# Third layer of a four-layer recurrent network: four PSUM banks for the attention scores, three for the ring

## The chip, the cores and the metric

The kernel runs on one core of a Trainium2 chip. The metric is the device time of one execution in microseconds (us). It stands for a whole network: four layers, each with an attention part and a feed-forward part, computed for four sequences ("rows") of 1024 tokens with 128 channels each.

PSUM, the memory that TensorE (PE) writes its products to, has eight banks per partition. One bank holds 128 x 512 float32 values, which is one product as this kernel makes them. ScalarE (ACT) and VectorE (DVE) read the banks. GpSimd (POOL) prepares masks and copies in SBUF.

## The reference, cut to what matters

The change touches the third layer. What it computes for each row `x` of 1024 tokens:

```python
xn = _layernorm(x, axis=-1)
s = _L2_attn_ref(xn, Wq, bq, Wk, bk, Wv, bv, Wo, bo, W1, b1, W2, b2, g1, beta1, g2, beta2)
g = _silu(_L2_ffn_ref(xn, gate_w, gate_b, w1, b1, w2, b2))
x = x + s * g

# the attention of _L2_attn_ref: 16 heads of 8 channels, full (no mask), rotary positions
q, k = apply_rope(heads(h @ Wq + bq)), apply_rope(heads(h @ Wk + bk))   # h: x normalised again
scores = q @ k.T / sqrt(8)
attn = softmax(scores) @ v

# _L2_ffn_ref: a switch layer, 8 experts with 80 places each
expert = argmax(softmax(tokens @ gate_w + gate_b))      # one expert for a token
dispatch = einsum('nec,nd->ecd', places, tokens)        # tokens into the experts' places
h = gelu(einsum('ecd,edf->ecf', dispatch, w1) + b1)
out = einsum('nec,ecd->nd', places * prob, einsum('ecf,efd->ecd', h, w2) + b2)
```

## The kernel before, in words

The first three layers each run `attention_layer`, which computes all four rows of a layer in one program for all engines. Nothing of its order is decided at run time. Each engine has several streams of work (generators); every item has a planned time, and `weave` puts the items of all streams of an engine into one sequence by these times. On the chip each engine then executes its sequence in order and waits on semaphores.

**Batches and blocks.** The heads of a row are taken in groups of four, and the queries in halves of 512, which makes 8 batches a row and 32 in the layer. A batch in the third layer has 8 blocks; a block is 128 keys against 512 queries, for four heads. For each head of a block PE makes a 128 x 512 product of scores in a bank of `ps_st`, ACT takes its exponential into `prob` (L1356), and PE multiplies `prob` with the values into the bank `ps_o` (L1254, eight matmuls for a block, "the values' product").

**Pairs.** The third layer uses a form of the operands in which two heads lie in different halves of PE's rows (`form.groups == 2`, in the code `paired`). PE works on two heads at a time where both are free to start. A pair of scores is four matmuls: two of L1267 (`score`) and two of L1274 (`score_apart`), which add the remaining terms. A block has two pairs; below they are called A (heads n = 0, 1) and B (n = 2, 3). The values' product of block b - 1 is planned between pair A and pair B of block b.

**Maxima.** The exponentials need the maximum of each query's scores, one batch ahead. PE computes the scores of the next batch once more the other way round (L1327, 128 queries x 512 keys, 32 of them for a batch, "fills", also in pairs), and DVE takes the maximum of each over its row (L1389, `TENSOR_REDUCE mhalf<-mx`). About four fills go with a block. After the last fill of a batch comes the turn of the maxima (L1339, kind "max"), and DVE makes three bf16 parts of it, which a DMA puts beside the queries (`qs<-neg`).

**The ring.** Fills share their banks, the tile `mx`, with everything else that PE makes for DVE or ACT in the meantime: the turned output of a batch (L1343, kind "out"), the arrival of the next row (L859, L685, L681), and the products of the switch layer (L1788 logits, L2460 counts, L2467 dispatch, L2474, L2486 hidden, L2495 second product, L2505 combination). All these products, in the order of their planned times, are the list `ring`; item i uses bank `i % RING`, and before it PE waits until item `i - RING` has been read (`open_bank`). The function `by` moves the reading of a switch product on DVE and ACT ahead of the planned time of item `slot + RING`, so that no engine waits for something behind itself.

**Scores' banks.** Score u (four for a block, counted through the layer) uses bank `u % 3` of `ps_st` and waits for the exponential of score u - 3 (`score_bank`). Both scores of a pair must be free before the two can run side by side.

Banks in the layer before: three for the scores, one for `ps_o`, four for the ring.

Of the kernel before, what the change touches and what calls it, by code (L numbers as in the profile page):

```python
# [20 lines left out]
ACT = mybir.ActivationFunctionType  # L21
# [3 lines left out]
P = 128  # L25
NT = T // P
HALF = 512
NH, DH = 16, 8
GH = 4
# [161 lines left out]
class Net:  # L191
# [32 lines left out]
    n = 0  # L224
# [160 lines left out]
PROBS = 3  # L385
# [612 lines left out]


NEG, NEG_NARROW = 5.0, 7.0  # L1000
RING = 4


def attention_layer(net, mode, scale, proj, ffns, arrivals=(), departures=()):
# [7 lines left out]
    nc = net.nc  # L1012
    rows = len(ffns)
    form = net.form
    R = form.rows
    paired = form.groups == 2
    heads_in_turn = (0, 2, 1, 3) if paired else (0, 1, 2, 3)
    batches = [(g, hf) for g in range(NG * rows) for hf in range(2)]
    NB = len(batches)
# [8 lines left out]
    for e, (g, hf) in enumerate(batches):  # L1028
        opens.append(len(blocks))
        for kt in range(NT):  # L1030
            lo, hi = queries_of(kt)
            q0, q1 = max(lo, hf * HALF), min(hi, (hf + 1) * HALF)
# [144 lines left out]
    with net.phase("att", names + proj.names + several) as (S, blk):  # L1177
        net.stale_next = net.stale_next + ffns[-1].used_up
        qs, ks, prob, vst, mhalf, mrow, neg, nrest, osb, rec = (net.qs, net.ks, net.prob, net.vst, net.mhalf, net.mrow, net.neg,
                                                                net.nrest, net.osb, net.rec)  # L1180
        ps_st = net.psum("ps_st", [P, 3, HALF])
        ps_o = net.psum("ps_o", [P, HALF])
        mx = net.psum("mx", [P, RING, HALF])
        proj.start(S, [ps_st[:, 0, :], ps_st[:, 1, :]], [mx[:, 2, :], mx[:, 3, :]], [ps_st[:, 2, :], ps_o[:, :]])
        proj.after = turn_max_at(0) + 1.1
        for r in range(rows):
            ffns[r].calm = [clock.at(y) + 0.8 for y in of_row[r][:-1]]
# [15 lines left out]
        def open_bank(pe, *item):  # L1203


            i = slot[item]
            if i >= RING:
                _, kind, e, n = ring[i - RING]
                if kind in FED:
                    sem, value = ffns[e].read(kind, n)  # L1210
                    pe.wait_ge(sem, value)
                else:
                    pe.wait_ge(S["mx_used"], place[kind, e, n])
            elif proj.rope and i >= 2:
                pe.wait_ge(S["s"], 1 + i)
            return mx[:, i % RING, :]

        for f in ffns:
# [24 lines left out]
        def scores(pe):  # L1243
# [12 lines left out]
                last.then_inc(S["summed"], 1)  # L1256

            def score_bank(u):
                if u >= 3:
                    pe.wait_ge(S["exped"], u - 2)  # L1260
                return ps_st[:, u % 3, :]

            def score(b, n, stop):
                e, kt, q0, q1 = blocks[b]
# [5 lines left out]
            def score_apart(b, n):  # L1270
                e, kt, q0, q1 = blocks[b]
                g = batches[e][0]
                row, lane = form.lane(heads_in_turn[n])
                return nc.tensor.matmul(ps_st[:, (GH * b + n) % 3, 0:q1 - q0], net.kx[row:row + 64, g % 2, lane, kt * P:(kt + 1) * P],  # L1274
                                        net.qx[row:row + 64, g % 2, q0:q1], start=False, stop=True)

            for b, (e, kt, q0, q1) in enumerate(blocks):
                for n in range(GH):
                    yield score_at(b, n)
                    if b == opens[e] and n == 0:  # L1280
                        pe.wait_ge(S["neg_landed"], negs * (e + 1))
                    if b == 0 and n == 0:
                        pe.wait_ge(S["value"], 4)
                        pe.wait_ge(S["vout"], 2)
                        if paired:
                            pe.wait_ge(S["apart"], 16 * 3 * GH)
                    if paired and n % 2 == 0:
                        score(b, n, False)
                        score(b, n + 1, False)
                        score_apart(b, n).then_inc(S["scores"], 1)  # L1290
                        score_apart(b, n + 1).then_inc(S["scores"], 1)
                    if not paired:
                        masks = score_masks(kt, q0, q1)
                        last = score(b, n, not masks)
                        for j, (m, a, z, c0, c1) in enumerate(masks):
                            last = nc.tensor.matmul(ps_st[:, (GH * b + n) % 3, c0:c1], net.ident_bf, m[:, a:z], start=False,  # L1296
                                                    stop=(j == len(masks) - 1))
                        last.then_inc(S["scores"], 1)
                    if n == (1 if paired else 3) and b >= 1:
                        yield values_at(b - 1)  # L1300
                        values(b - 1)
# [44 lines left out]
        def exponentials(act):  # L1346
            for b, (e, kt, q0, q1) in enumerate(blocks):
                for n, h in enumerate(heads_in_turn):
                    u = GH * b + n
                    yield score_at(b, n)  # L1350
                    act.wait_ge(S["scores"], u + 1)
                    if u == 0:
                        act.wait_ge(S["p3"], 4)
                    if n == 0 and b >= PROBS:
                        act.wait_ge(S["summed"], b - PROBS + 1)
                    nc.scalar.activation(prob[:, b % PROBS, h, 0:q1 - q0], ps_st[:, u % 3, 0:q1 - q0], ACT.Exp,  # L1356
                                         scale=scale).then_inc(S["exped"], 1)
                if b >= 1 and b - 1 == closes[blocks[b - 1][0]]:
                    yield from take_output(act, blocks[b - 1][0])
            yield from take_output(act, NB - 1)  # L1360
# [2424 lines left out]
```

## Time and profile before

| | us |
|---|---|
| median of 3 runs (lowest, highest) | 4225.28 (4214.74, 4245.58) |
| the profiled execution | 4225.9 |
| its span | 4223.9 |
| PE, DVE, ACT, POOL busy in the span | 3664.7, 2647.4, 2149.2, 864.8 |

The page of the profile gives the busy time of each engine in the span. Of the lines named above, it lists L1356 (ACT), L1389 (DVE), L1327, L1267 and L1254 (PE) as the five costliest groups of the program; the first two layers use them too. In the third layer the scores run from 1720.7 to 2800.2 us. The rows further down are all from there. In a row of the timeline the first number is the start, the second the length of a merged run of like instructions, `x2` their count, and the bracket at the end says how long the engine sat idle before them and which instruction ended that.

### The profile page before, as it was taken

Reading aid. Unit: us, or ns where it says so; the run is one execution under the profiler, and the core shown is the slowest. Engines: PE = TensorE matmul, PEld = TensorE weight load, DVE = VectorE, ACT = ScalarE, POOL = GpSimd, SP = SyncE. Lnnn points to the kernel's source line nnn. Section 1 sums busy time; section 2 is a strip of 40 time slices with the busy share of each in tenths; the row PEclk is TensorE's granted clock in tenths of the full one; section 3 lists DMA queues with packets and bytes.
Section 4 is the critical chain, followed back from the end, with each engine's and each line's share of the span. In section 5 each row is a group of like instructions: output and inputs, shape, how many; then the busy total and the mean of one; then the engine's idle time right before and its main releaser. Section 6 shows DMA issues by size and latency. Waiting matters only on the chain. (4 is left out here: it accounts for less than half of the span.)

```text
span 4223.9 us, 77424 instructions
## 1 busy us (share of the span) xinstructions
PE 3664.7 (87%) x28760; PEld 2040.5 (48%) x28760; DVE 2647.4 (63%) x5977; ACT 2149.2 (51%) x4957; POOL 864.8 (20%) x1071
## 2 busy tenths in 40 slices
PE   5988978888989995899898898989888898888987
PEld 3655654444545543333333333345555665555565
DVE  5667646565555654777677777737555665665765
ACT  3555554554555453465565655653554554444454
POOL 1111000000010002122233132124212331431421
PEclk8999988988999898899999999999999999999999
DMA  3212311101101102111011011002120230321212
GB/s 111 61 46 43 75 27 46 40 22 44 24 18 44 29 13 85 35 32 39 18 44 32 24 39 32 23 31 63 36 72 23 61 81 8 80 60 29 56 41 54
DMA packets 149533, 183.37 MB, mean 43 GB/s; under 512 B 34568, under 2 KB 102216, under 8 KB 145832
## 3 DMA queue, kind: packets, MB, share of 16 engines
q1 hardware_dynamic: 143268, 171.01, 15.5%
q10 hardware_dynamic: 5892, 7.41, 0.7%
q8 instruction: 230, 3.77, 0.4%
q14 instruction: 143, 1.17, 0.1%
HBM read 91.69 MB, written 34.08 MB: 30 GB/s over the span
## 5 line engine op out<-in xcount | busy, mean ns | idle before, releaser
L1356 ACT ACTIVATE prob<-ps_st 128x512 f32<-128x512 f32 (+3 forms) x2432 | 1123.5, 510 | 1146.6 <-PE ps_st L1296 577.9
L1389 DVE TENSOR_REDUCE mhalf<-mx 128x1 f32<-128x512 f32 (+3 forms) x2064 | 1256.7, 653 | 589.1 <-PE mx L1330 316.5
L1327 PE MATMUL mx<-ks,qs 56*128 56x512 bf16 (+4 forms) x2304 | 648.7, 365 | 125.9 <-DVE g_tok L1964 52.6
L1267 PE MATMUL ps_st<-qs,ks 59*128 59x512 bf16 (+4 forms) x2432 | 678.1, 350 | 82.5 <-ACT prob L1356 69.9
L1254 PE MATMUL ps_o<-prob,vst 128*32 128x512 f32 (+3 forms) x5376 | 566.7, 504 | 2.7 <-ACT osb L1367 1.5
L1267 PEld LDWEIGHTS ps_st<-qs,ks 75*128 75x128 bf16 (+1 forms) x2432 | 206.3, 98 | 504.9 <-ACT prob L1356 356.0
L1327 PEld LDWEIGHTS mx<-ks,qs 72*128 72x128 bf16 (+1 forms) x2304 | 199.9, 100 | 390.5 <-DVE mhalf L1389 86.4
L1439 POOL COPY vst<-v_tok 128x256 f32<-128x256 f32 x48 | 19.8, 416 | 1137.9 <-PE ps_o L1254 1137.4
L3312 ACT ACTIVATE o<-ps,nm,lrq 128x128 f32<-128x128 f32 x512 | 227.1, 459 | 35.3 <-DVE nm L3427 24.0
L1274 PE MATMUL ps_st<-qx,kx 64*128 64x512 bf16 x1024 | 241.7, 386 | 0.0
L1254 PEld LDWEIGHTS ps_o<-prob,vst 128*32 128x32 f32 x5376 | 113.8, 110 | 165.7 <-issue 65.9
L2377 POOL TENSOR_SCALAR ffn_small<-bcs,table 80x128 f32<-80x128 f32 x256 | 148.6, 598 | 124.4 <-PE mx L2505 113.5
L2022 PE MATMUL mx<-stream 128*128 128x128 f32 x1024 | 155.1, 294 | 0.4 <-DVE mhalf L1389 0.2
L2022 PEld LDWEIGHTS mx<-stream 128*128 128x128 f32 x1024 | 138.3, 203 | 31.0 <-issue 21.7
L1296 PE MATMUL ps_st<-band_kq_bf,ident_bf 128*128 128x128 bf16 (+2 forms) x1024 | 149.7, 218 | 0.0
L3380 DVE SCALAR_TENSOR_TENSOR o<-ps,stream,tabs 128x512 f32<-128x512 f32 x128 | 94.6, 744 | 67.3 <-ACT ctx_tok L3282 27.1
L1330 PE MATMUL mx<-band_qk_bf,ident_bf 128*128 128x134 bf16 (+2 forms) x960 | 134.7, 222 | 0.0
L1995 PE MATMUL mx<-xn_ch,stream 128*128 128x512 f32 x256 | 120.7, 619 | 4.3 <-ACT stream L1981 4.3
L3093 PE MATMUL ps<-xn_ch,stream 128*128 128x512 f32 x256 | 120.9, 594 | 3.5 <-DVE xn_ch L3368 3.5
L253 PE MATMUL pt<-ident_bf 128*128 128x512 bf16 x336 | 95.7, 423 | 28.7 <-ACT o L3312 28.7
L1296 PEld LDWEIGHTS ps_st<-band_kq_bf,ident_bf 128*128 128x128 bf16 x1024 | 102.3, 100 | 26.2 <-issue 7.6
L1296 PE MATMUL ps_st<-later_kq_bf,ident_bf 128*128 128x128 bf16 x512 | 112.2, 233 | 0.0
(488 smaller groups left out, 6563.1 us busy)
## 6 DMA issues: line engine op xcount, KB each, us to landing
qs<-q_scr SPq DMA_DIRECT2D x186, 96.0 KB
ks<-k_scr SPq DMA_DIRECT2D x90, 192.0 KB
lkt<-o SPq DMA_DIRECT2D x256, 64.0 KB, 2.0
lve<-lv SPq DMA_DIRECT2D x24, 512.0 KB, 4.6
lqt<-o SPq DMA_DIRECT2D x160, 64.0 KB, 2.0
tabs<-local_tables SPq DMA_DIRECT2D x4, 2048.0 KB, 8.6
k_scr<-part SPq DMA_DIRECT2D x30, 256.0 KB, 3.2
lqt<-o ACTq DMA_DIRECT2D x96, 64.0 KB, 2.1
```

The source lines that it names most:

```text
L1254: last = nc.tensor.matmul(ps_o[32 * h:32 * h + 32, a - hf * HALF:z - hf * HALF], vst[:, g % 2, kt, h, :], prob[:, b % PROBS, h, a - q0:z - ...
L1267: return nc.tensor.matmul(score_bank(GH * b + n)[:, 0:q1 - q0], ks[g % 2][row:row + R + 3, lane, kt * P:(kt + 1) * P], qs[g % 2][row:row + ...
L1274: return nc.tensor.matmul(ps_st[:, (GH * b + n) % 3, 0:q1 - q0], net.kx[row:row + 64, g % 2, lane, kt * P:(kt + 1) * P], net.qx[row:row + ...
L1296: last = nc.tensor.matmul(ps_st[:, (GH * b + n) % 3, c0:c1], net.ident_bf, m[:, a:z], start=False, stop=(j == len(masks) - 1))
L1327: last = nc.tensor.matmul(bank[:, j * w:(j + 1) * w], qs[g % 2][row:row + R, hf, lane, (t - 4 * hf) * P:(t - 4 * hf + 1) * P], ks[g % 2][r ...
L1330: last = nc.tensor.matmul(bank[:, j * w + c0:j * w + c1], net.ident_bf, m[:, a:z], start=False, stop=(k == len(masks) - 1))
L1356: nc.scalar.activation(prob[:, b % PROBS, h, 0:q1 - q0], ps_st[:, u % 3, 0:q1 - q0], ACT.Exp, scale=scale).then_inc(S["exped"], 1)
L1389: nc.vector.tensor_reduce(mhalf[:, hf, h0:h0 + heads, t - 4 * hf, part], bank[:, 0:heads * (k1 - k0)].rearrange("p (n w) -> p n w", n=head ...
L2022: last = nc.tensor.matmul(bank[:, t * C:(t + 1) * C], self.h[:, i, j, t * P:(t + 1) * P], W(f"l1_w2_{e}", self.HB, j), start=(j == 0), sto ...
L2377: last = nc.gpsimd.tensor_scalar(self.sec_t[:, t % 2, e, :], self.bcs[:, t * P:(t + 1) * P], net.K("slot_id")[0:CAP, e:e + 1], None, ALU.i ...
L3093: last = nc.tensor.matmul(pab[:, n % 2, s, :], W(f"l3_wqkv{d}")[:, c0:c0 + P], ch[:, i * HALF:(i + 1) * HALF], start=True, stop=True)
L3312: nc.scalar.activation(pr[:, g, i, :], ps[:, t % 2, g, i, :], ACT.Exp, bias=nm[:, g, i:i + 1], scale=norm[t][:, i // 2, g, i % 2:i % 2 + 1 ...
```

## The change

In the third layer, and only there (`paired`), the scores get four banks and the ring three; the first two layers keep three and four. Of the projection's second products, one moves from `mx` into the fourth bank of `ps_st`. The first use of the third bank of `mx` and the first score wait until all four of these products have been read (`S["s"]`, 4).

```diff
-RING = 4
+BANKS = 7
...
+    SB = 4 if paired else 3
+    RING = BANKS - SB
...
-        ps_st = net.psum("ps_st", [P, 3, HALF])
+        ps_st = net.psum("ps_st", [P, SB, HALF])
         ps_o = net.psum("ps_o", [P, HALF])
         mx = net.psum("mx", [P, RING, HALF])
-        proj.start(S, [ps_st[:, 0, :], ps_st[:, 1, :]], [mx[:, 2, :], mx[:, 3, :]], [ps_st[:, 2, :], ps_o[:, :]])
+        proj.start(S, [ps_st[:, 0, :], ps_st[:, 1, :]], [ps_st[:, 3, :], mx[:, 2, :]] if paired else [mx[:, 2, :], mx[:, 3, :]], [ps_st[:, 2, :], ps_o[:, :]])
...
             elif proj.rope and i >= 2:
-                pe.wait_ge(S["s"], 1 + i)
+                pe.wait_ge(S["s"], 4 if paired else 1 + i)
             return mx[:, i % RING, :]
...
             def score_bank(u):
-                if u >= 3:
-                    pe.wait_ge(S["exped"], u - 2)
-                return ps_st[:, u % 3, :]
+                if u >= SB:
+                    pe.wait_ge(S["exped"], u - SB + 1)
+                return ps_st[:, u % SB, :]
...
                         if paired:
                             pe.wait_ge(S["apart"], 16 * 3 * GH)
+                            pe.wait_ge(S["s"], 4)
...
-                    nc.scalar.activation(prob[:, b % PROBS, h, 0:q1 - q0], ps_st[:, u % 3, 0:q1 - q0], ACT.Exp,
+                    nc.scalar.activation(prob[:, b % PROBS, h, 0:q1 - q0], ps_st[:, u % SB, 0:q1 - q0], ACT.Exp,
                                          scale=scale).then_inc(S["exped"], 1)
```

PE, ACT, POOL and SP keep the order of their instructions. On DVE `by` now looks three items ahead, so that some readings of switch products move forward past one or two reductions, or past the reading of an "out". DVE's order in the second row, around the first dispatch copy (L2417; in the changed kernel the same instruction is L2420, L1389 is L1392, L1415 and L1421 are L1418 and L1424). Before:

```order
L1389 TENSOR_REDUCE mhalf<-mx 128x1 x12
L1415 RECIPROCAL rec<-mx 128x16
L1421 TENSOR_TENSOR tabs<-mx,rec 128x4x32
L2417 COPY ffn_small<-mx 128x160
L1389 TENSOR_REDUCE mhalf<-mx 128x1 x8
```

With the change:

```order
L1392 TENSOR_REDUCE mhalf<-mx 128x1 x12
L2420 COPY ffn_small<-mx 128x160
L1418 RECIPROCAL rec<-mx 128x16
L1424 TENSOR_TENSOR tabs<-mx,rec 128x4x32
L1392 TENSOR_REDUCE mhalf<-mx 128x1 x8
```

The copy moved ahead of the two readings of the turned output, because the "out" is now the item that needs the copy's bank.

PE's order at the start of the layer, where the projection's second products (L444) are made. Before:

```order
L442 MATMUL ps_st<-in_ch,w 128x512
L444 MATMUL mx<-in_ch,w 128x512
L442 MATMUL ps_st<-in_ch,w 128x512
L444 MATMUL mx<-in_ch,w 128x512
L442 MATMUL ps_st<-in_ch,w 128x512
```

With the change:

```order
L442 MATMUL ps_st<-in_ch,w 128x512
L444 MATMUL ps_st<-in_ch,w 128x512
L442 MATMUL ps_st<-in_ch,w 128x512
L444 MATMUL mx<-in_ch,w 128x512
L442 MATMUL ps_st<-in_ch,w 128x512
```

Every other second product goes to the new bank of `ps_st`; nothing changed its place.

## Rows read from the trace of the kernel before

**Rows 1.** Busy time by engine, 1720 to 2815 us; granted clock, DMA share, GB/s last.

```profile
1720.00:2815.00 1095.00, 988.59 (x6760) 372.29 (x6761) 763.51 (x1591) 642.35 (x1244) 278.29 (x428) 0.98 0.11 33
```

**Rows 2.** Waits, same stretch: who waited for whom, total us, times, longest.

```profile
PE ps_st L1267 <- ACT prob L1356: 49.1, 139, 3.1
...
ACT prob L1356 <- PE ps_st L1274: 490.0, 322, 53.0
```

**Rows 3.** Timeline, one block with four fills and nothing else.

```profile
2126.10 0.39 PE L1267 MATMUL ps_st<-qs,ks 59*128 59x512 bf16 x2
...
2126.54 0.38 PE L1327 MATMUL mx<-ks,qs 56*128 56x512 bf16 x2
2126.74 1.09 ACT L1356 ACTIVATE prob<-ps_st 128x512 f32<-128x512 f32 x2 [0.46 <-PE ps_st L1274]
2126.76 0.38 PE L1267 MATMUL ps_st<-qs,ks 59*128 59x512 bf16 x1
2126.96 2.58 DVE L1389 TENSOR_REDUCE mhalf<-mx 128x1 f32<-128x512 f32 x4 [0.46 <-PE mx L1327]
2127.39 0.39 PE L1267 MATMUL ps_st<-qs,ks 59*128 59x512 bf16 x1 [0.25 <-ACT prob L1356]
...
2127.62 0.59 PE L1327 MATMUL mx<-ks,qs 56*128 56x512 bf16 x2
...
2128.14 1.07 PE L1254 MATMUL ps_o<-prob,vst 128*32 128x512 f32 x8
...
2129.14 0.39 PE L1267 MATMUL ps_st<-qs,ks 59*128 59x512 bf16 x2
```

**Rows 4.** Timeline, one block of the last batch, which has no fills.

```profile
2791.75 0.39 PE L1267 MATMUL ps_st<-qs,ks 59*128 59x512 bf16 x2
...
2793.04 0.39 PE L1267 MATMUL ps_st<-qs,ks 59*128 59x512 bf16 x1 [0.47 <-ACT prob L1356]
...
2793.58 1.07 PE L1254 MATMUL ps_o<-prob,vst 128*32 128x512 f32 x8
2794.57 0.39 PE L1267 MATMUL ps_st<-qs,ks 59*128 59x512 bf16 x2
```

**Rows 5.** Timeline, one block with six fills, four of them together.

```profile
1762.87 0.39 PE L1267 MATMUL ps_st<-qs,ks 59*128 59x512 bf16 x2
...
1763.73 3.18 DVE L1389 TENSOR_REDUCE mhalf<-mx 128x1 f32<-128x512 f32 x5 [0.47 <-PE mx L1327]
...
1764.39 1.07 PE L1327 MATMUL mx<-ks,qs 56*128 56x512 bf16 x4
1765.40 1.07 PE L1254 MATMUL ps_o<-prob,vst 128*32 128x512 f32 x8
1766.40 0.39 PE L1267 MATMUL ps_st<-qs,ks 59*128 59x512 bf16 x2
```

**Rows 6.** Timeline, a dispatch product's copy behind an "out" (second row).

```profile
2021.03 1.29 DVE L1389 TENSOR_REDUCE mhalf<-mx 128x1 f32<-128x512 f32 x2 [2.47 <-PE mx L1327]
2021.93 0.66 PE L1343 MATMUL mx<-table,osb 128*128 128x128 f32 x4
...
2023.12 0.31 DVE L2417 COPY ffn_small<-mx 128x160 f32<-128x160 f32 x1
...
2023.49 0.39 PE L1327 MATMUL mx<-ks,qs 56*128 56x512 bf16 x2 [0.37 <-DVE ffn_small L2417]
```

**Rows 7.** Line L1327, same stretch as Rows 1: what ended PE's idle time before.

```profile
  DVE mhalf L1389: 30.3, 79
  DVE tabs L2433: 29.5, 36
  DVE xn_ch L2426: 15.9, 29
```

**Rows 8.** Timeline, a row's arrival (square root on ACT), and after a hidden window.

```profile
2056.42 0.60 PE L1267 MATMUL ps_st<-qs,ks 59*128 59x512 bf16 x1 [3.12 <-ACT prob L1356]
...
2148.67 0.39 PE L1267 MATMUL ps_st<-qs,ks 59*128 59x512 bf16 x1 [1.30 <-ACT prob L1356]
```

More of the change, by code:

```diff
@@ L1273, in score_apart @@
                 row, lane = form.lane(heads_in_turn[n])
-                return nc.tensor.matmul(ps_st[:, (GH * b + n) % 3, 0:q1 - q0], net.kx[row:row + 64, g % 2, lane, kt * P:(kt + 1) * P],
+                return nc.tensor.matmul(ps_st[:, (GH * b + n) % SB, 0:q1 - q0], net.kx[row:row + 64, g % 2, lane, kt * P:(kt + 1) * P],
                                         net.qx[row:row + 64, g % 2, q0:q1], start=False, stop=True)
@@ L1295, in scores @@
                         for j, (m, a, z, c0, c1) in enumerate(masks):
-                            last = nc.tensor.matmul(ps_st[:, (GH * b + n) % 3, c0:c1], net.ident_bf, m[:, a:z], start=False,
+                            last = nc.tensor.matmul(ps_st[:, (GH * b + n) % SB, c0:c1], net.ident_bf, m[:, a:z], start=False,
                                                     stop=(j == len(masks) - 1))
```

## The prediction

> **What bounds the kernel now.** I read the busy time by engine over the third layer first, then the waits of PE and ACT there, then the timeline of single blocks, and last what ends PE's idle time before the fills. Only the third layer changes. In its 1095 us PE is busy for 989, DVE for 764 and ACT for 642 [rows 1]. PE is the engine nearest to its limit, but its busy time does not show how many matmuls ran side by side. The waits show where banks are short: a score waited for an exponential 139 times, 49.1 us in all, and ACT in turn waited 490.0 us for scores [rows 2]. The two wait for each other in a loop.
>
> The loop is read in a block that has only its four fills [rows 3]. I count from the start of pair B, 2126.10. B's fills start at 0.44. ACT starts B's two exponentials at 0.64 and is through at 1.73. The first score of pair A starts at 0.66, the second only at 1.29, when the first exponential has ended (1.19) and 0.10 has passed. A's fills follow at 1.52, the second of them 0.21 later (0.59 for two of 0.38), the values' product at 2.04, the next pair B at 3.04. The 0.63 between the two scores of A is what the missing bank costs: A0 runs alone for 0.38, then PE idles for 0.25. The values' product takes 1.00 and starts 0.31 after the last fill.
>
> **The fourth bank.** With it the second score of A needs an exponential that is long past, so A runs as a pair at 0.66 and its fills could start at 1.10. But the values' product needs B's exponentials, ready at 1.73 + 0.10 = 1.83. The last batch shows that loop without any fills: there the second score of A waits as well, and the values' product starts at 2793.58 - 2791.75 = 1.83 and the next block at 2.82 [rows 4]. So a block can't go below 2.83, and of the 0.63 given back at A only 0.21 is left where the block is plain. In blocks where a product of the switch layer or of the arrival stands between A and the values' product, exponentials are done in time and the whole 0.63 is returned.
>
> **The third ring bank.** A pair of fills (i, i + 1) needed the reads of i - 4 and i - 3, both of the pair before last. Now its second fill needs the read of i - 2, the first fill of the pair just before. In the plain block DVE starts the first read at 0.86 and needs 2.58 / 4 = 0.645 for each [rows 3]; PE goes on 0.06 after a read (2023.12 + 0.31 to 2023.49, [rows 6]). The second of A's fills can thus start at 0.86 + 0.645 + 0.06 = 1.57, the values' product at 1.88, the next block at 2.88 in place of 3.04. DVE needs 2.58 of these, so it keeps up. **Gain 0.16 a block; by my count over the layer's timeline 58 blocks are of this kind: 9.3 us.**
>
> **Blocks with other work behind A.** I count 35 in which A split by 0.63 and neither the exponentials nor the ring hold the values' product afterwards: 35 x 0.63 = 22 us. In 21 more a part comes back, about 0.35 each: 7.4 us. Together with the plain ones these are 114 blocks, against 139 waits [rows 2].
>
> **Blocks with four fills in a row.** I count 46, about half behind pair A and half behind pair B. In the one shown, A's fills start at 1.52, all four run through, and the values' product starts at 2.53, the next block at 3.53 [rows 5]. With three banks the four fills follow the reads one by one. DVE reads B's fills from 0.86 to 2.15 and A's first to 2.80; A's second fill starts at 1.57, the third at 2.15 + 0.06 = 2.21, the fourth at 2.80 + 0.06 = 2.86, the values' product at 3.17. That is 0.64 later than before, in a block that before also had its 0.63 split: all of that is already set off. Worked out for four fills behind B I get the same, one read more. It isn't made up later, since the following block without fills was held by the exponentials anyway. **Loss 46 x 0.64 = 29 us.**
>
> **Switch and arrival products.** Behind a long product, the first fill of a pair now waits for its read instead of the second; they then start together, which costs nothing. It costs where a single item follows. The "out" of 2021.93 used a free bank; now it must wait for the copy, which DVE takes up behind two reductions: 2021.03 + 1.29 + 0.31 + 0.06 = 2022.69, 0.76 later [rows 6]. The bound from below is nothing (the earlier start of PE covers it), from above one read and a copy, 0.96. I take 0.65 and 20 such places: **13 us**. The eight windows of hidden products lose a bank as well, and a fill behind them waits for one more GELU, but ACT must first load the table for the exponentials, which held the second score of A for 1.30 [rows 8]: nothing. If that cover were gone, 0.9 each, 7 us.
>
> **Arrivals.** While ACT works on the square root of an arriving row, PE stands for 3.12 us [rows 8]. With four banks pair B and its fills pass before PE stops, some 0.65 to 1.3 us earlier in the end; three arrivals, 3 us.
>
> **The start of the layer.** The third fill bank and the first score wait for the last sine product's read; the keys' transfers that the fills need come later. Nothing.
>
> Sum: -9.3 - 22 - 7.4 - 3 + 29 + 13 = +0.3. In one stretch of five blocks that I worked through in turn the result was 0.1 us slower, where the terms above give about zero, because a PE that is earlier meets the same DVE; I add 2 us. Against the profiled execution of 4225.9, which lies 0.6 above the median of the runs, this gives **4228 us, no change.**
>
> **Rivals.**
>
> *Faster, the fourth bank pays and the ring has slack* (0.15). DVE is idle for 30% of the layer [rows 1], and its lag behind PE may be taken up by an earlier start of the fills. Then the 29 and 13 us shrink to a few, and what is left is 42 plus the 0.05 a plain block in which the ring and not the exponentials decides (3): 4225.9 - 45 = 4181. Against it: at 79 fills PE already stood until DVE's reduction with four banks [rows 7]. It holds if fewer than about 15 of the 46 blocks lose a read.
>
> *All of the split comes back* (0.03). Every one of the 139 waits returns its idle time and the 0.38 in which one score ran alone: 49.1 + 139 x 0.38 = 102, 4124 us. Against it speak the blocks of the last batch [rows 4], whose period the bank doesn't set. The Trainium skill has this as its rule: "Perfetto Trace Analysis", Optimization Strategy, takes the same gap repeating on the engine that should be saturated as a sign that SBUF or PSUM is too small for the next tile. By it the sum would be the 102 us; the trace agrees with it on where the gap is and, in the last batch, not on its worth.
>
> *Slower, the ring becomes the bound* (0.20). PE's idle time before a fill was ended 79 times by a reduction, 36 times by the reading of a combination product and 29 times by that of a second product [rows 7]. If every one of these 144 places waits for one more read, each before a values' product, the loss is 144 x 0.645 = 93 us in place of 42, less the 42 gained: 4225.9 + 51 = 4277. It decides where DVE is behind by a read or more when a pair of fills comes. It speaks for this rival that a stall splits the pair of fills, so that they run one after the other; against it, that such a pair was mostly split before, and then nothing is added.
>
> *Neither bank matters* (0.05): the exponentials' loop holds everywhere and DVE's lag is absorbed: 4226.
>
> **Chances.** The forecast itself has 0.57. A change within 1%, 42 us, is what I call no change, about what a measurement of this kernel can tell. Faster by over 1%: 0.15, most of the two faster cases. Slower by over 1%: 0.20. Within: 0.65. The range goes from the first faster case to the slower one, 4180 to 4275.
>
> **What the profile after would show.** Waits of scores for exponentials nearly gone, pairs A at 0.66 behind B; plain blocks at 2.88; four fills in a row spread over some 1.3 us more, with waits for DVE's reductions before L1327 up several times; the blocks of the last batch still at 2.82. I am wrong if plain blocks stay at 3.04 or go to 2.83 with four fills unspread, or if the waits before fills exceed what the scores gave back by more than 40 us.

## The result, and the profile after

The changed kernel takes 4264.27 us (median of 9 runs, 4255.67 to 4278.19), the kernel before 4229.10 beside it (9 runs, 4212.58 to 4245.58). The ratio is 1.0088, 95% interval 1.0066 to 1.011: slower by 0.9%, 35 us. The forecast was 4228, no change. By the prediction's bound of 1% it is no change, but the interval shows a loss, and the time lies nearer to the slower rival (4277) than to the forecast. One execution of all those below, of the first kernel with short reads, took 10497 us at a mean granted clock of 0.388 and is left out of every time.

The profiled execution after has a span of 4257.0, against 4223.9. I cut the third layer of both traces into its 255 blocks, from one pair A to the next. Their sum is 30.7 us longer (1077.2 before), and the layer's start lies 2.3 later, so the two differ where the change was made. Busy time by engine as in [rows 1], over the layer's blocks from its first pair A:

```profile
1723.02:2830.92 1107.90, 972.95 (x6696) 374.52 (x6698) 757.59 (x1565) 620.99 (x1229) 274.74 (x426) 0.97 0.11 33
```

PE is idle for 1107.90 - 972.95 = 135 us of the layer. The same view of the kernel before, from its first pair A:

```profile
1720.68:2797.85 1077.17, 977.08 (x6696) 366.51 (x6696) 758.05 (x1566) 633.40 (x1229) 275.80 (x426) 0.98 0.12 33
```

There it was idle for 100. So 35 us of idle time were added and 4 of busy time went. Who waited for whom after, as [rows 2] (L1267 has become L1269, L1274 L1276, L1254 L1256, L1327 L1330, L1356 L1359, L1389 L1392; PEld is PE's weight load):

```profile
PEld mx L1330 <- DVE mhalf L1392: 136.4, 230, 1.8
...
PE mx L1330 <- DVE mhalf L1392: 35.2, 96, 1.3
```

Before, the scores' wait for exponentials stood there with 139 times and 49.1 us. Now it is the fills that wait, 96 times for 35.2 us. A matmul of a fill had waited for a reduction only this often:

```profile
PE mx L1327 <- DVE mhalf L1389: 2.3, 11, 0.2
```

The exchange is plainest in the idle time before each matmul line (busy and mean | idle before, and what ended it). Before, from 1720 to 2815:

```profile
L1254 PE MATMUL ps_o<-prob,vst 128*32 128x512 f32 x2048 | 281.4, 622 | 2.7 <-ACT osb L1367 1.5 <-ACT prob L1356 1.2
L1267 PE MATMUL ps_st<-qs,ks 59*128 59x512 bf16 x1024 | 271.6, 391 | 53.7 <-ACT prob L1356 49.1 <-DMA qs<-neg 3.2 <-DVE mhalf L1389 1.1
L1327 PE MATMUL mx<-ks,qs 56*128 56x512 bf16 x984 | 241.3, 387 | 32.7 <-DVE tabs L2433 9.5 <-DVE bcs L2422 6.3 <-DVE ffn_small L2417 4.3
```

and after, from 1720 to 2831, since the layer now ends later:

```profile
L1256 PE MATMUL ps_o<-prob,vst 128*32 128x512 f32 x2032 | 281.6, 627 | 16.7 <-ACT prob L1359 13.2 <-ACT osb L1370 3.5
L1330 PE MATMUL mx<-ks,qs 56*128 56x512 bf16 x988 | 266.8, 392 | 90.8 <-DVE mhalf L1392 35.2 <-DVE tabs L2436 13.9 <-DVE xn_ch L2429 9.3
L1269 PE MATMUL ps_st<-qs,ks 59*128 59x512 bf16 x1022 | 209.6, 393 | 5.4 <-DMA qs<-neg 3.2 <-ACT prob L1359 1.9
```

The scores gave back 53.7 - 5.4 = 48.3. The fills took 90.8 - 32.7 = 58.1, and the values' products 16.7 - 2.7 = 14.0. The same view gives 6.1 before the hidden products (L2489) and 4.2 before the "out" (L1346), where it gave 0.2 and 0.8 before. Together that is 33 of the 35 us. Line L1330, what ended the idle time before its matmuls and weight loads, where [rows 7] had 79, 36 and 29 times:

```profile
  DVE mhalf L1392: 171.6, 326
  DVE tabs L2436: 40.5, 36
  DVE xn_ch L2429: 27.7, 26
```

**The plain block** [rows 3], rows of PE and of its weight load:

```profile
2135.54 0.39 PE L1269 MATMUL ps_st<-qs,ks 59*128 59x512 bf16 x2
...
2136.21 0.38 PE L1269 MATMUL ps_st<-qs,ks 59*128 59x512 bf16 x2
...
2136.65 0.89 PE L1330 MATMUL mx<-ks,qs 56*128 56x512 bf16 x2
2137.15 0.09 PEld L1330 LDWEIGHTS mx<-ks,qs 56*128 56x128 bf16 x1 [0.62 <-DVE mhalf L1392]
...
2137.47 1.06 PE L1256 MATMUL ps_o<-prob,vst 128*32 128x512 f32 x8
...
2138.47 0.39 PE L1269 MATMUL ps_st<-qs,ks 59*128 59x512 bf16 x2
```

Pair A runs undivided at 0.67 behind B. A's first fill starts at 1.11, the second waits for a read, the values' product starts at 1.93 and the next pair B at 2.93. It was 3.04.

**Four fills in a row** [rows 5]. This pair B began at 1735.97:

```profile
1737.08 0.89 PE L1330 MATMUL mx<-ks,qs 56*128 56x512 bf16 x2
1737.58 0.09 PEld L1330 LDWEIGHTS mx<-ks,qs 56*128 56x128 bf16 x1 [0.62 <-DVE mhalf L1392]
1738.18 0.09 PEld L1330 LDWEIGHTS mx<-ks,qs 56*128 56x128 bf16 x1 [0.51 <-DVE mhalf L1392]
...
1738.77 0.09 PEld L1330 LDWEIGHTS mx<-ks,qs 56*128 56x128 bf16 x1 [0.50 <-DVE mhalf L1392]
...
1739.10 1.06 PE L1256 MATMUL ps_o<-prob,vst 128*32 128x512 f32 x8
1740.09 0.39 PE L1269 MATMUL ps_st<-qs,ks 59*128 59x512 bf16 x2
```

One fill now follows each read, 0.6 apart. The values' product stands at 3.13 where it stood at 2.53, the next pair B at 4.12 (3.53). Over the layer, the 46 blocks with four fills in a row hold 59 of the waits of a fill for a reduction, with 22.9 of the 35.2 us; before they held one, of 0.2.

**The last batch** [rows 4], without fills:

```profile
2827.69 0.39 PE L1269 MATMUL ps_st<-qs,ks 59*128 59x512 bf16 x2
...
2829.47 1.06 PE L1256 MATMUL ps_o<-prob,vst 128*32 128x512 f32 x8 [0.73 <-ACT prob L1359]
2830.47 0.39 PE L1269 MATMUL ps_st<-qs,ks 59*128 59x512 bf16 x2
```

2.78 from B to B, where it was 2.82: the exponentials hold it, and the wait only moved from the score to the values' product.

**An "out"** [rows 6] now waits for the copy ahead of it (first row below). **An arrival** [rows 8], where the longest wait had been 3.12, now has two waits of 1.34 and 0.51:

```profile
2033.13 0.66 PE L1346 MATMUL mx<-table,osb 128*128 128x128 f32 x4 [0.61 <-DVE ffn_small L2420]
...
2067.39 0.39 PE L1330 MATMUL mx<-ks,qs 56*128 56x512 bf16 x1 [1.34 <-DVE mhalf L1392]
...
2068.28 0.88 PE L1269 MATMUL ps_st<-qs,ks 59*128 59x512 bf16 x2 [0.51 <-ACT prob L1359]
```

**A hidden window.** PE now stands inside it:

```profile
2154.13 1.28 ACT L2451 ACT_TABLE_LOAD   x1
...
2156.46 1.88 PE L2489 MATMUL mx<-ffn_small,stream 128*128 128x80 f32 x8 [1.47 <-ACT ffn_small L2451]
...
2159.26 1.93 PE L1256 MATMUL ps_o<-prob,vst 128*32 128x512 f32 x8
```

There are four hidden products in a window, and a GELU for each. With three banks the fourth uses the bank of the first, so it waits for the first GELU, and that comes behind a table load. Afterwards the values' product takes 1.93 and not 1.06. The granted clock (third number from the end) in and behind this window shows why it is longer:

```profile
2152.00:2157.00 5.00, 3.53 (x29) 3.30 (x28) 1.04 (x2) 4.97 (x12) 1.16 (x1) 0.96 0.05 12
2157.00:2159.00 2.00, 2.00 (x9) 1.33 (x8) 0.08 (x1) 2.00 (x11) 1.15 (x1) 0.50 0.00 0
2159.00:2161.00 2.00, 2.00 (x9) 0.20 (x8) 1.20 (x2) 1.82 (x4) 0.00 (x0) 0.50 0.00 0
2161.00:2163.00 2.00, 2.00 (x14) 0.74 (x11) 0.38 (x1) 0.81 (x2) 0.00 (x0) 0.50 0.00 0
```

Of PE's two levels, 2.4 and 1.2 GHz, it had the lower for some 6 us from the end of the stall on. The block took 10.81 us; in the kernel before the same block took 8.28, at a clock of 1.00 throughout.

By kind of block, before to after, in us:

| kind (its make-up before) | blocks | difference (each rounded) |
|---|---|---|
| four fills in a row | 46 | +26.4 |
| four fills in two pairs, nothing else | 93 | +6.1 |
| one with only the turn of the maxima | 10 | -0.9 |
| with hidden products | 8 | +8.7 |
| all others (other products, "out", last batch) | 98 | -9.5 |
| sum | 255 | +30.7 |

Two of the three blocks in which an arriving row's square root stops PE have the make-up of plain ones and stand among the 93, the third stands among the 46.

### The profile page after: what moved, and what is told of

It reads as the page before. It is cut to its first block and busy times, and to the rows that moved or that the text cites. A ratio compares the mean times of both kernels' runs of the same rounds, so it can differ in the third digit from the quotient of the medians.

```text
span 4257.0 us, 77424 instructions
## 1 busy us (share of the span) xinstructions
PE 3661.3 (86%) x28760; PEld 2049.0 (48%) x28760; DVE 2646.9 (62%) x5977; ACT 2135.6 (50%) x4957; POOL 863.6 (20%) x1071
## 5 line engine op out<-in xcount | busy, mean ns | idle before, releaser
L1359 ACT ACTIVATE prob<-ps_st 128x512 f32<-128x512 f32 (+3 forms) x2432 | 1110.0, 512 | 1187.7 <-PE ps_st L1299 573.3
L1392 DVE TENSOR_REDUCE mhalf<-mx 128x1 f32<-128x512 f32 (+3 forms) x2064 | 1251.3, 651 | 618.5 <-PE mx L1333 317.8
L1330 PE MATMUL mx<-ks,qs 56*128 56x512 bf16 (+4 forms) x2304 | 673.1, 367 | 183.9 <-DVE g_tok L1967 52.0
L1269 PE MATMUL ps_st<-qs,ks 59*128 59x512 bf16 (+4 forms) x2432 | 616.3, 350 | 35.0 <-ACT prob L1359 22.7
L1256 PE MATMUL ps_o<-prob,vst 128*32 128x512 f32 (+3 forms) x5376 | 567.7, 505 | 18.6 <-ACT prob L1359 15.1
L1330 PEld LDWEIGHTS mx<-ks,qs 72*128 72x128 bf16 (+1 forms) x2304 | 199.8, 100 | 514.1 <-DVE mhalf L1392 199.5
L1269 PEld LDWEIGHTS ps_st<-qs,ks 75*128 75x128 bf16 (+1 forms) x2432 | 190.2, 98 | 377.1 <-ACT prob L1359 211.4
L1276 PE MATMUL ps_st<-qx,kx 64*128 64x512 bf16 x1024 | 207.0, 387 | 0.0
L1256 PEld LDWEIGHTS ps_o<-prob,vst 128*32 128x32 f32 x5376 | 113.9, 110 | 164.6 <-issue 67.8
L3383 DVE SCALAR_TENSOR_TENSOR o<-ps,stream,tabs 128x512 f32<-128x512 f32 x128 | 94.5, 743 | 67.2 <-ACT ctx_tok L3285 27.3
L253 PE MATMUL pt<-ident_bf 128*128 128x512 bf16 x336 | 95.2, 421 | 29.6 <-ACT o L3315 29.6
L1333 PEld LDWEIGHTS mx<-band_qk_bf,ident_bf 128*128 128x128 bf16 x960 | 96.5, 101 | 31.6 <-issue 5.7
```

What stands on the lines that cost most here:

```text
L1256: last = nc.tensor.matmul(ps_o[32 * h:32 * h + 32, a - hf * HALF:z - hf * HALF], vst[:, g % 2, kt, h, :], prob[:, b % PROBS, h, a - q0:z - ...
L1269: return nc.tensor.matmul(score_bank(GH * b + n)[:, 0:q1 - q0], ks[g % 2][row:row + R + 3, lane, kt * P:(kt + 1) * P], qs[g % 2][row:row + ...
L1276: return nc.tensor.matmul(ps_st[:, (GH * b + n) % SB, 0:q1 - q0], net.kx[row:row + 64, g % 2, lane, kt * P:(kt + 1) * P], net.qx[row:row + ...
L1330: last = nc.tensor.matmul(bank[:, j * w:(j + 1) * w], qs[g % 2][row:row + R, hf, lane, (t - 4 * hf) * P:(t - 4 * hf + 1) * P], ks[g % 2][r ...
L1333: last = nc.tensor.matmul(bank[:, j * w + c0:j * w + c1], net.ident_bf, m[:, a:z], start=False, stop=(k == len(masks) - 1))
L1392: nc.vector.tensor_reduce(mhalf[:, hf, h0:h0 + heads, t - 4 * hf, part], bank[:, 0:heads * (k1 - k0)].rearrange("p (n w) -> p n w", n=head ...
```

## The experiments

The kernel before ran beside each group of them (medians of 17 to 23 runs: 4227.28, 4227.56, 4226.31 us); ratios are to those runs. A single trace can differ from the median, since layers 1 and 2, which are the same code, end between 1705 and 1736 us in these traces. So times are compared by ratio, and the traces only by the blocks of layer 3.

### The change taken apart: the ring alone, the order alone

The ring of three alone. The eighth bank holds nothing but products of the projection at the start (against the changed kernel, cut to the sizes):

```diff
-    SB = 4 if paired else 3
-    RING = BANKS - SB
+    SB = 3
+    RING = 3 if paired else 4
```

> The third layer with three banks for the scores and three for the ring; the eighth bank holds nothing but two of the projection's sine products. The engines' orders are those of the changed kernel, so against the changed kernel this takes away the fourth score bank alone, and against the kernel before it shows the ring alone. Theory (the ring of three costs, the fourth score bank returns little, because the exponentials and the reads of the fills hold the values' product anyway): the split of pair A is back (about 139 waits), and the time is 15 to 35 us above the changed kernel, 1.2 to 1.7% above before. Rival (the two effects are separate and each large): the ring alone costs 33 + 68 = 100 us, 2.4% above before. Rival (the fourth bank returns nothing at all): the same time as the changed kernel within 5 us.

Measured: 4285.01 us, ratio 1.0131 (1.0114 to 1.0149). That is 21 us above the changed kernel, as the theory had it.

The order alone: four ring banks and three for scores, but DVE's readings placed as for a ring of three (against the kernel before; ACT's order stays as it was):

```diff
-        i = slot[item] + RING
+        i = slot[item] + (3 if paired else RING)
```

> The kernel before with its banks (three and four), but with the look-ahead of the order set to three in the third layer, so that DVE has the order of the changed kernel: some readings of switch products come one or two reductions earlier. Theory (the missing bank costs, not the order): within 3 us of before. Rival (DVE now waits for switch products with reductions behind it, and that is the loss): 15 to 33 us slower.

Measured: 4214.11 us, ratio 0.9971 (0.9956 to 0.9986). This is slightly faster than the kernel before, which I had not seen coming.

The three traces add up over the layer's blocks as follows:

| step | four fills | plain | max | hidden | other | sum | by medians |
|---|---|---|---|---|---|---|---|
| order for a ring of three | -3.3 | -3.9 | 0.0 | +1.4 | -1.4 | -7.2 | -13 |
| ring of three | +38.1 | +12.7 | -0.5 | +12.1 | +8.2 | +70.6 | +71 |
| fourth score bank | -8.5 | -2.7 | -0.4 | -4.8 | -16.3 | -32.7 | -21 |

So the ring bank is worth two to three and a half times the score bank, whose worth is known only beside a ring of three. The score bank gives half its gain in blocks with other work and next to nothing in plain ones. In the run with the ring alone (1718 to 2861 us) both waits stand side by side:

```profile
PE ps_st L1270 <- ACT prob L1360: 44.5, 140, 2.7
PE mx L1331 <- DVE mhalf L1393: 28.2, 81, 0.8
```

### Is it the length of DVE's reads?

Both kernels, with DVE reading 256 of the 512 columns, so that half of the keys are left out of the maxima:

```diff
-                                            bank[:, 0:heads * (k1 - k0)].rearrange("p (n w) -> p n w", n=heads),
+                                            bank[:, 0:256].rearrange("p (n w) -> p n w", n=1) if paired else
+                                            bank[:, 0:heads * (k1 - k0)].rearrange("p (n w) -> p n w", n=heads),
```

> The kernel before, but in the third layer each of DVE's reductions reads 256 of the 512 columns of its bank, so that half of the keys are left out of the maxima; a read takes about 0.38 us instead of 0.645. It is the base for the next kernel. Theory (DVE's reads set the pace at the places with four fills and behind the long products): 20 to 40 us faster than before. Rival (the loop of scores and exponentials alone sets the pace with four ring banks): within 10 us of before.

> The changed kernel with the same short reads (half of the keys left out of the maxima). Against the short-read version of before it shows the change where the ring has slack. Theory (the loss is DVE's reads against three banks): the loss turns into a gain, 15 to 45 us faster than the short-read version of before, with plain blocks at 2.83 us. Rival (the loss comes from something else that the change brings, the order or the clock): still 15 us or more slower than the short-read version of before.

Measured: 4174.83 us with the banks before (median of six; 0.9871, 0.9851 to 0.9891) and 4176.58 with the changed banks (0.988, 0.9866 to 0.9895). The first gained more than the 20 to 40 us expected. With short reads the change costs nothing, so its loss of 35 us hangs for the most part on the time of the reads. But it doesn't gain the 15 to 45 us of the theory either. To see why, one more execution of the first, for its trace:

> The run with short reads on the banks before, once more for its trace (it leaves half the keys out of the maxima). Its time was 4178 against 4177 on the changed banks. Theory 1 (with short reads the score bank's gain is there, and what eats it is waits for products' copies and GELUs, which are not shortened): plain blocks stay at 3.04 against 2.83 on the changed banks, and the changed banks lose as much in blocks with products and hidden windows, 8 us or more in the latter. Rival (with short reads the fills get through so early that the split of A no longer sets anything): plain blocks at 2.83 here as well.

Measured: 4167.17 us in one run. A read now took 418 ns instead of 684. Idle time before the lines, short reads, banks before, from 1711 us, where this layer starts:

```profile
L1389 DVE TENSOR_REDUCE mhalf<-mx 128x1 f32<-128x256 f32 x984 | 366.2, 418 | 349.6 <-PE mx L1327 346.5 <-DVE neg L1408 1.5
L1254 PE MATMUL ps_o<-prob,vst 128*32 128x512 f32 x2048 | 277.0, 613 | 3.1 <-ACT osb L1367 1.8 <-ACT prob L1356 1.2
L1267 PE MATMUL ps_st<-qs,ks 59*128 59x512 bf16 x1024 | 272.7, 388 | 56.3 <-ACT prob L1356 46.1 <-DMA qs<-neg 6.0 <-DVE mhalf L1389 3.8
...
L1327 PE MATMUL mx<-ks,qs 56*128 56x512 bf16 x984 | 223.9, 383 | 17.5 <-DVE tabs L2434 4.3 <-DVE bcs L2423 4.2 <-ACT ffn_small L2449 4.2
```

and short reads with the changed banks:

```profile
L1256 PE MATMUL ps_o<-prob,vst 128*32 128x512 f32 x2048 | 278.0, 615 | 25.7 <-ACT prob L1359 15.5 <-ACT osb L1370 7.1
L1330 PE MATMUL mx<-ks,qs 56*128 56x512 bf16 x992 | 245.2, 388 | 41.7 <-DVE tabs L2437 10.1 <-DVE mhalf L1392 9.0 <-DVE xn_ch L2430 6.5
L1269 PE MATMUL ps_st<-qs,ks 59*128 59x512 bf16 x1024 | 208.6, 390 | 8.2 <-DMA qs<-neg 6.3 <-ACT prob L1359 1.6
```

The scores give back 48.1. The fills lose 24.2, most of it no longer to reductions but to the copies and sums of products, which were not shortened, and the values' products lose 22.6, mostly to the exponentials. By kind, from the banks before to the changed ones: four fills +7.2, plain -4.1, hidden +8.1, other -19.3, max -0.3, sum -8.5. The typical plain block went from 3.04 to 2.78, the hidden windows still lost 8. The first theory stands in these two points, but not in the blocks with other products, which gained 19. The sum of -8.5 is one trace against one, while the medians differ by 2; in part it can be the clock, since the layer had the lower level for 25 us in the first trace and for 37 in the second.

### Four fills in a row, taken apart

Fills dealt out at three places of a block instead of two, on the changed banks, on those before, and on those before with the look-ahead of three, which gives the same order as the first:

```diff
-            return clock.at(starts[b] + (0.5 * int(2 * (at - starts[b]) / lasts[b]) + 0.22) * lasts[b])
+            return clock.at(starts[b] + (0.22, 0.45, 0.72)[int(3 * (at - starts[b]) / lasts[b])] * lasts[b])
```

> The banks of the changed kernel; fills are dealt out at three places of a block instead of two, so that four in a row no longer occur. Theory 1 (the loss of the ring of three lies in the 46 blocks with four fills in a row, 0.57 us each): 26 us come back, 4238 us, and PE's waits for DVE's reductions before the fills fall from 96 to under 40. Rival (each pair of fills anywhere pays one read, since DVE reads a fill in 0.645 and the ring holds no more than one and a half reads): the waits stay at 90 or more, and the time is within 8 us of the 4264 of the changed kernel.

> The same three places for the fills, with the banks of the kernel before. Theory 1 (with four banks a run of four fills costs nothing): within 8 us of the kernel before, 4220 to 4236. Rival (spreading by itself gives 10 us or more, as fills then stand between B's scores and A's): 4217 or less; what the thirds do on three banks would then have to be counted less this gain.

> The banks of the kernel before, fills at three places of a block, and the order made with a look-ahead of three: instruction for instruction the order of the run with thirds on the changed banks, so the two differ by their banks alone. The same pair without thirds lies 50 us apart (4214 and 4264). Theory 1 (some 26 us of that are the blocks with four fills in a row): the pair with thirds lies 15 to 30 us apart, this kernel at 4222 to 4236. Rival (the read of the newest pair is paid in whatever block it falls): the pair lies 40 to 50 apart, this kernel at 4201 to 4211, and it would be the fastest.

Measured: 4250.74, 4243.07 and 4226.48 us. The first came down from 4264 by half of what its theory said (4238), the second missed its range (4220 to 4236), and the third lies within that of its theory. As ratios, with two places for comparison:

| fills at | banks before | banks before, order of three | changed banks |
|---|---|---|---|
| two places | 1 | 0.9971 (0.9956 to 0.9986) | 1.0088 (1.0066 to 1.011) |
| three places | 1.0034 (1.0017 to 1.0052) | 0.9996 (0.9981 to 1.0011) | 1.0045 (1.0028 to 1.0062) |

At one order the banks cost 0.0117, 50 us, where four fills stand in a row, and 0.0049, 24 us by the medians (4226.48 to 4250.74; 21 by the ratios), where they don't. In the traces the layer's blocks differ by 37.9 and 13.6. Between the second and the third column the 46 blocks cost 29.6 us with two places and 1.9 with three. This is the size that the prediction gave them. The waits of a fill for a reduction in these blocks fell from 59 to 9, and those in the whole layer to

```profile
PE mx L1330 <- DVE mhalf L1392: 20.3, 61, 1.8
```

which is more than the 40 times that I had expected. The others stand in blocks of other kinds: a single pair pays a read too at times. Spreading by itself costs 14 us with four banks. So both the theory and its rival hold in part, by 26 us and by 21 to 24.

### Work between the pairs instead of a bank

Fills of a block's first half ahead of pair A, with the banks before; and the same with the order of three (the second edit is the look-ahead above):

```diff
-            return clock.at(starts[b] + (0.5 * int(2 * (at - starts[b]) / lasts[b]) + 0.22) * lasts[b])
+            return clock.at(starts[b] + (-0.03, 0.72)[int(2 * (at - starts[b]) / lasts[b])] * lasts[b])
```

> The banks of the kernel before; the fills of a block's first half are put ahead of pair A, right behind B's own. Theory 1 (what the fourth score bank gives is only cover for one exponential, and work put between B and A gives it as well): in a plain block the four fills run first, A's second score finds its exponential done at 1.29, the values' product starts at 1.83, and the block takes 2.83 instead of 3.04; of 139 waits of scores for exponentials fewer than 40 are left; over some 150 blocks that is 15 to 30 us: 4200 to 4212. Rival (four fills behind each other run into the reads of DVE with four banks too): A starts only when the fourth fill has gone, A's exponentials are late, and the values' product of the NEXT block waits; waits before fills rise from 79 to over 120 and the time is 4225 or more.

> As the run with fills ahead of pair A, and with the order of fills and products made as for a ring of three, while four banks are there (the order alone gave 0.9971 of the time before). Theory 1 (the two gains lie in different blocks and add up): 4190 to 4202. Rival (both give the same idle time back): the better of the two alone, 4205 to 4214.

Measured: 4287.06 us (1.0129, 1.0094 to 1.0164) and 4278.05 (1.0118, 1.008 to 1.0156). The rival held in both. In the trace of the first, scores waited for exponentials 30 times instead of 139, and the blocks that had been plain took 9.8 us less in sum, but those with other work took 59.4 more. Fills behind each other ran into DVE's reads with four banks too, 79 times where it had been 11, and the turn of the maxima (L1339), which needs the last fill's read, came too close behind it:

```profile
PE mx L1339 <- DVE mrow L1394: 29.0, 16, 3.2
PE mx L1327 <- DVE mhalf L1389: 27.4, 79, 1.0
PE ps_st L1267 <- ACT prob L1356: 24.4, 30, 3.8
```

The layer was at the lower clock level for 122 us in this trace and for 47 in that of the kernel before. If the same matmuls take up to twice as long there (the values' product above took 1.93 for 1.06), these 75 us are at most 37 of the layer's 67 us. How much of the loss is waits alone was not separated.

### The hidden windows

In the four windows in which the values' product came behind the hidden products, it now runs before the fourth one (against the changed kernel; then the same on the banks before, with the look-ahead of three):

```diff
     def values_at(b):
+        if paired:
+            for m in [m for f in ffns for m in f.marks]:
+                if starts[b + 1] <= m <= starts[b + 1] + 0.3 * lasts[b + 1]:
+                    return clock.inside(m, 0.62)
         return clock.at(starts[b + 1] + (0.3 if paired else 0.65) * lasts[b + 1])
```

> The changed kernel, with one thing moved: in four of the eight windows of hidden products the values' product runs before the fourth hidden product instead of behind it and the fills. In the changed kernel PE stood there 1.47 us for the GELU of the first, behind ACT's table load of 1.28, and was then granted half its clock for some 6 us in two windows (10.82 us each, 8.28 before). Theory 1 (stall and clock are the loss in these windows): the values' product of 1.07 fills the stall, the clock stays at 1.00, the two long windows fall to 8.3 to 9.0, all four by 5 to 6 us, the time to 4258. Rival (the exponentials that wait for the second table load set the end of the window whatever PE does): the windows keep their length to 0.5 us, and the time 4264.

> The banks of the kernel before, look-ahead of three, and the values' product inside the four windows of hidden products. Theory 1 (the order's gain of 0.3% and the windows' are apart; with four ring banks a fill waited 1.01 for a GELU in the windows and the values' product stood behind it): 4 x 0.8 = 3 us less than the 4214 of the order alone, 4211, ratio 0.9965. Rival (with four banks the window ends with ACT's work): 4214.

Measured: 4249.32 us (1.0063, 1.0045 to 1.0082) and 4220.05 (0.9987, 0.9975 to 1). On the changed banks the two long windows went from 10.81 to 8.26 each, at full clock:

```profile
2145.00:2147.00 2.00, 1.88 (x16) 0.89 (x15) 0.00 (x0) 1.97 (x6) 0.26 (x1) 1.00 0.00 0
2147.00:2150.00 3.00, 1.89 (x13) 1.27 (x14) 0.69 (x1) 3.00 (x15) 1.15 (x1) 1.00 0.00 0
```

PE still waits for the GELU there, 0.47 instead of 1.47, and 0.27 and 0.48 more before the fills behind it. But another of the four grew from 7.89 to 10.93, now at half clock itself:

```profile
1846.00:1849.00 3.00, 2.98 (x18) 2.98 (x19) 1.71 (x4) 2.44 (x6) 0.00 (x0) 0.66 0.38 105
1849.00:1852.00 3.00, 3.00 (x16) 2.36 (x19) 0.00 (x0) 1.57 (x7) 0.00 (x0) 0.50 0.34 107
```

The layer's blocks together were 1.5 us longer than in the changed kernel. By the ratios the time was some 10 us shorter, but the interval meets that of the changed kernel, and the trace doesn't show the gain in this layer. On the banks before nothing was gained over the order alone (4214.11, where 4211 was expected). That the two long windows lose through stall and clock together is shown; how the loss divides between the two is not, nor that moving one item cures the layer.

## Why the prediction was right and wrong

The time was within the range and within 1%, but the balance of +2 was wrong: the layer's blocks came to +31. A range of 95 us carried the forecast, not the sum. The prediction does not list its blocks, so its terms are set here beside the kinds of block, with the three blocks of the arrivals taken out of their kinds:

| term | forecast | came to |
|---|---|---|
| plain blocks | -9.3 | +8.6 |
| blocks with other work, products | -22 - 7.4 + 13 = -16.4 | -9.5 |
| four fills in a row | +29 | +27.3 |
| hidden windows | 0 | +8.7 |
| arrivals | -3 | -3.5 |
| turn of the maxima | none | -0.9 |
| added for an earlier PE meeting the same DVE | +2 | |
| sum | +2.3 | +30.7 |

- **The wait for the exponentials goes: right.** PE's 139 waits and 49.1 us became 3 and 1.9, though 24 waits and 13.2 us for exponentials now stand before the values' products, where there had been one of 1.2.
- **Plain block 2.88 in place of 3.04: right in kind, a gain of 0.11 and not 0.16.** The block came to 2.93: its values' product started 0.05 later than I had put it. The floor of the exponentials is there, 2.78 in the last batch. What failed is the count, "58 blocks are of this kind: 9.3 us". Of the 93 blocks, 19 had taken 3.02 to 3.06, and 16 of these fell by 0.06 to 0.12. But 18 of the 93 grew by over 0.3, 12.6 us in sum, and the whole kind by 6.1 (8.6 without the two arrivals). 14 of the 18 stand right behind a block with other products. In the 18, the matmuls of fills waited 7.4 us for the readings of such products, where it had been 3.0, and 2.4 for reductions, where it had been nothing. An example is the block whose pair A starts at 2204.24. Its second fill waited 1.12 for the reading of a combination product:

```profile
2204.69 0.38 PE L1330 MATMUL mx<-ks,qs 56*128 56x512 bf16 x1
2206.19 0.39 PE L1330 MATMUL mx<-ks,qs 56*128 56x512 bf16 x1 [1.12 <-DVE tabs L2436]
```

  It took 3.93, where it had taken 2.96. The ring doesn't end at a block's edge. I counted within blocks.
- **35 x 0.63 + 21 x 0.35 = 29 gained behind other work, 13 lost at products: too good by 7.** The short reads show how much of this is DVE's: with them the same kind gained 19.3.
- **Four fills, 46 x 0.64 = 29 lost: right.** 26.4 in the trace (27.3 without the arrival), 29.6 at one order, and 1.9 when the fills were dealt out otherwise. In the block shown, the values' product came 0.60 later, not 0.64.
- **Hidden windows, nothing: wrong.** They lost 8.7, of which 5.1 in the two long ones. I had looked for the wait at the fill behind the window and found it covered by the second table load. It arose inside, at the fourth hidden product, at 1.47 behind the first table load, and in two windows the clock fell after it. My price for the lost cover, 7, was near by luck: it was set on a wait behind the window, and the loss arose inside.
- **Arrivals, -3: right.** The three blocks went from 6.95, 6.90 and 6.56 to 5.96, 5.47 and 5.47: -3.5.
- **The moved readings: not priced.** They gave 0.29% by themselves.
- **[rows 7] was read wrong.** Its 79, 36 and 29 count the matmuls of fills and their weight loads together. PE's matmuls alone waited 11, 12 and 9 times, 32 places and not 144, and 2.3 us in all for reductions. So "at 79 fills PE already stood" was no evidence against a ring with slack, and the slower rival's price rested on the same count.
- **Which rival came nearest:** that the ring becomes the bound. Its test, that waits before fills exceed what the scores gave back by more than 40 us, was not met (58.1, or 72.1 with the values' products, against 48.3), and the price of one read in all 144 places was too high. But the idle time now lies where it said. The rule on bubbles that the prediction took from the Trainium skill ("Perfetto Trace Analysis", Optimization Strategy) finds the gap. It names no price; with the 102 us that the prediction worked out for it the fourth score bank compares badly, at 21 to 33. Taking the bank from the ring cost 71.

**A version ahead of both.** The look-ahead of three alone, with the banks before, took 0.9971 of the time before. A pair with the fills at three places points the same way (1.0034 to 0.9996); in the pair with the fills ahead of pair A the difference (1.0129 to 1.0118) is within the intervals. It makes DVE read a product of the switch layer ahead of a reduction or two. Its gain in the traces, 7.2 us here and 13.6 in the pair with three places, lies mostly in plain blocks and those with four fills in a row, and I have not shown which readings carry it.

## What to carry to other kernels

- When a fixed number of banks is divided between two rings, price both in one unit, the idle time before the matmuls of each. The longer list of waits (139 against 11) was that of the less valuable bank; the waits of the other appeared only when it was taken away. Count the waits of the matmuls apart from those of the weight loads.
- A bank of a loop that is also held by its reader's work gives back at most the difference to that reader's own period. Here a plain block went from 3.04 to 2.93, or to 2.78 with short reads, while the split was 0.63. A bank of the ring cost about one read (0.60 in the block shown) where four products stood in a row for three banks.
- Ask for every place in which a ring serves a second engine, and follow the ring over the edges of the blocks: here four GELUs behind a table load.

## What was unexpected of the hardware

- PE's granted clock fell to its lower level at the end of PE's stall of 1.47 us in two hidden windows. In the kernel before, a stall of 1.01 us in the same window (2145 us) left it at 1.00. In the run with the values' product inside, it fell at 1847 us behind waits of only 0.57 and twice 0.21. So these traces don't show that the length of the one stall decides it.
- From the first pair A of the layer to the last, PE had the lower level for 47 us before and for 65 after; over all the traces here it was 25 to 122. At up to twice the time for the same matmuls the 18 us more are at most 9 of the 31. 12 of the 18 lie in the two hidden windows. I had no term for it.
- Where the lower level comes changed from kernel to kernel with small moves of work, as in the window above. A difference of a few us between two orders can be this and nothing else.
